# Counting edges with constant tile counts, and attention weights with sources on partitions, in a two-layer graph network

## The reference

```python
h = relu(layernorm(x))
Wh = h @ W.T + b_W;  s_s = Wh @ a_src;  s_d = Wh @ a_dst
e  = leaky_relu(s_s[src] + s_d[dst] + a_b, 0.2)
attn = softmax of e over the edges of each dst
h_prime = segment_sum(attn * Wh[src], dst) + h @ res_W.T + res_b
x = x + gru(h_prime, h)
h = relu(layernorm(x))
for _ in range(4):
    a = segment_sum((h @ W_edge[type].T + b_edge[type])[src], dst)
    h = gru(a, h)
x = x + h
```

## Time and profile before

| | us |
|---|---|
| median of 3 runs | 458.15 (457.98 to 459.03) |
| profiled execution | 458.77 |
| its span, first to last instruction | 456.9 |
| TensorE busy in the span | 391.9 (86%) |
| VectorE busy | 265.6 (58%) |
| ScalarE busy | 160.6 (35%) |
| POOL busy | 98.9 (22%) |

### The profile page before, as it was taken

How to read it: one execution, slowest core, us unless ns; L and a number is a source line. 1 busy time by engine, 2 the same in 40 slices (tenths; PEclk the granted TensorE clock), 3 DMA queues, 4 the chain that set the end, 5 groups by cost and what they waited for, 6 DMA issues and landing times.

```text
span 456.9 us, 8180 instructions
## 1 busy us (share of the span) xinstructions
PE 391.9 (86%) x2544; PEld 280.3 (61%) x2544; DVE 265.6 (58%) x746; ACT 160.6 (35%) x339; POOL 98.9 (22%) x124
## 2 busy tenths in 40 slices
PE   1468856888888889978889999999999999999994
PEld 0365534657777779865337567475674656746693
DVE  6979886776666662576845544444454444544234
ACT  3522118434564654744322232222222222222022
POOL 2101000000000000001007760067700677005500
PEclk9969957888998999999999999999999999999999
DMA  6200000000000000001221331123321233202201
GB/s 154 49 1 1 0 1 0 1 2 1 2 1 2 2 1 1 1 1 47 93 98 47 102 93 71 47 64 99 98 76 47 61 100 100 75 31 74 65 3 32
DMA packets 14500, 19.93 MB, mean 44 GB/s; under 512 B 2591, under 2 KB 7728, under 8 KB 14460
## 3 DMA queue, kind: packets, MB, share of 16 engines
q1 hardware_dynamic: 10276, 12.90, 8.1%
q0 software_dynamic: 2912, 5.97, 5.2%
q10 hardware_dynamic: 1272, 0.54, 0.4%
HBM read 8.27 MB, written 11.13 MB: 42 GB/s over the span
## 4 chain that ended last, share of the span: by engine, by line
PE 72%; DVE 12%; issue 6%; ACT 5%; DVEq 4%; DMA 0%; POOL 0%; SPq 0%; ACTq 0%; POOLq 0%
PE small L1583 26%; PE big L1565 7%; PE small L1447 6%; PE big L1430 6%; PE small L1466 5%; DVE cell_hot L930 3%; PE small L1604 2%; PE small L1617 1%; PE big L1528 1%; DVEq L309 1%; PE small L1528 1%; PE big L1530 1%; PE big L1529 1%; PE small L1519 1%; PE small L1530 1%
## 5 line engine op out<-in xcount | busy, mean ns | idle before, releaser
L1583 PE MATMUL small<-nibbles,store 128*128 128x384 fp8e4 (+1 forms) x640 | 125.8, 353 | 1.4 <-DVE store L1107 0.8
L462 POOL DMA_INDIRECT scores<-messages,w_gat x91 | 88.2, 969 | 120.1 <-DMA messages<-store 93.5
L1583 PEld LDWEIGHTS small<-nibbles,store 128*128 128x128 f16 x640 | 62.3, 98 | 64.4 <-issue 7.3
L930 DVE TENSOR_SCALAR cell_hot<-iota,cell_w,fields 128x320 bf16<-128x320 f16 x264 | 75.1, 357 | 17.1 <-PE big L1430 7.7
L1430 PE MATMUL big<-cell_hot,store 128*128 128x320 bf16 x264 | 56.5, 342 | 20.1 <-DVE cell_hot L930 15.9
L1430 PEld LDWEIGHTS big<-cell_hot,store 128*128 x264 | 35.6, 145 | 36.5 <-issue 32.0
L693 ACT CAST store<-digit_words 128x512 f16<-128x512 f32 x40 | 24.6, 618 | 82.2 <-DVE digit_words L1103 82.2
L1103 DVE TENSOR_TENSOR digit_words<-big,edge_rows 128x512 f32<-128x512 f32 x40 | 27.4, 690 | 40.7 <-PE big L1565 40.7
L1565 PE MATMUL big<-wT,h 128*128 128x512 f32 x80 | 38.6, 599 | 3.0 <-ACT h L689 2.9
L448 POOL TENSOR_TENSOR rstd<-var_e,power 128x2 f32<-128x2 f32 x5 | 3.5, 695 | 140.7 <-DVE var_e L1091 140.7
L1046 DVE SCALAR_TENSOR_TENSOR cell_hot<-rz,cell_hot 128x256 f32<-128x256 f32 (+2 forms) x29 | 11.0, 380 | 38.0 <-ACT cell_hot L664 38.0
(11 more groups left out here) (269 smaller groups left out, 551.8 us busy)
## 6 DMA issues: line engine op xcount, KB each, us to landing
messages<-store SPq DMA_DIRECT2D x40, 256.0 KB, 2.0
scores<-messages,w_gat POOLq DMA_INDIRECT x91, 2.5
xn<-in_x SPq DMA_DIRECT2D x1, 576.0 KB
out<-xn SPq DMA_DIRECT2D x4, 128.0 KB
store<-in_edge_attr SPq DMA_DIRECT2D x1, 256.0 KB
wn<-in_L_gnn_W_edge SPq DMA_DIRECT2D x1, 256.0 KB, 6.4
wn<-in_L_gnn_Wi ACTq DMA_DIRECT2D x1, 192.0 KB, 3.9
wn<-in_L_gnn_Wh_g ACTq DMA_DIRECT2D x1, 192.0 KB, 6.1
```

The costliest lines, as they stand in the source:

```text
L462: g.indirect_dma_start(out=rows16[:, u].rearrange("p a f -> p (a f)"), out_offset=None, in_=table_rows[s % 2][:], in_offset=bass.IndirectO ...
L930: last = v.tensor_scalar(half_hot[:, b * GROUP + q], iota[:, b * HALF:(b + 1) * HALF], cell_w[:, half, bass.ds(tile + q, 1)], fields[:, 1, ...
L1583: last = mm(bank[:, 0:w], m16[s % 2][:, i, t, part], A8[:, t % 2, i, lo:lo + w, t // 2], start=(i == 0 and part == 0 and t == 0), stop=(i ...
```

## The change

The tile count of each of the 40 half windows is now a constant (`TILES`, 231 in all); only the starts are still read from the data, one word for a turn of four half windows. One-hots and matmuls are written out without loops; the ring of eight runs on from half to half; the zero matmuls are gone (the first and last matmul of a half open and close it), and ScalarE's evacuation waits for the count of matmuls (`K.slot`). `cell_w` has four sets instead of two and is filled earlier. `count_turn` swaps the sides: the identity is stationary, digits move in spans of 512 columns, and counts come out with sources on partitions. `weigh` works on sources on partitions, in ten pieces of 128 columns, from `fall` (one column per target, made by a matmul of a new `b_cols`, a Relu and an exponential) and `s_tall` (one number per source). Its result is the stationary side of `aggregate` directly: prob turn and its copy are gone in the fast path. Aggregate J-2 runs in turn J (before, J-3), weigh J-2 right after digits J-1, and the tail is re-ordered to match.

Removed lines that the print above shows are left out where there are more than two on end.

```diff
+TILES = (27, 13, 10, 9, 8, 7, 7, 7, 6, 6, 6, 6) + 8 * (5,) + 2 * (5, 4) + 15 * (4,) + (1,)
+HOTS_BEFORE = (0, *accumulate(TILES))
+AHEAD = 63
+CELL_SETS = 4
...
+        def tile_ranges(eng, J):
+            word = eng.value_load(table[0:1, J:J + 1], min_val=0, max_val=(1 << 26) - 1)
+            first = eng.snap(word & 255)
+            starts = [first]
+            for shift in (8, 14, 20):
+                starts.append(eng.snap(first + ((word >> shift) & AHEAD)))
+            return (starts[0:2], starts[2:4])
+        def window_hots(j, starts):
+            for b, first in enumerate(starts):
+                before = HOTS_BEFORE[2 * j + b]
+                for lo in range(0, TILES[2 * j + b], 2):
+                    tiles = [nc.s_assert_within(first + u, 0, ETP - 1, skip_runtime_bounds_check_because=
+                                                "a start plus its tiles ends within ETP")
+                             for u in range(lo, min(lo + 2, TILES[2 * j + b]))]
+                    yield b, before + lo, tiles
...
+        def weights(n):
+            return exp_b if isinstance(n, int) and n % 2 else exp_a
...
+            for n, run in groupby(range(NS), lambda w: TILES[w]):
+                run = list(run)
+                g.memset(limits[:, run[0]:run[-1] + 1], float(ETP - n)).then_inc(C.limits, len(run))
...
-                act.wait_ge(K.window, 2 * J + half + 1)
+                act.wait_ge(K.slot, HOTS_BEFORE[2 * (2 * J + half + 1)])
...
-            def window_cells(j, half):
-                a.activation(cell_w[:, half], fields[:, 2], ACT.Copy, bias=-float(CELLS * j)).then_inc(K.cellw, 1)
+            def window_cells(j):
+                a.activation(cell_w[:, j % CELL_SETS], fields[:, 2], ACT.Copy,
+                             bias=-float(CELLS * j)).then_inc(K.cellw, 1)
...
-                    if there(J):
-                        window_cells(2 * J + 1, 1)
+                    if 2 * J + 3 < NW:
+                        window_cells(2 * J + 3)
                 if there(J - 3):
...
+                    attn_out(J - 3, J - 3)
+                if J == 1:
+                    falls()
                 if there(J):
                     evac(J, 0)
-                if there(J + 1):
-                    window_cells(2 * J + 2, 0)
+                if 2 * J + 4 < NW:
+                    window_cells(2 * J + 4)
                 if there(J - 1):
                     counts_out(J - 1, count_sum[:, J - 1:J])
                     excesses(J - 1)
+            def falls():
+                act.wait_ge(S0.s_fall, 1)
+                act.wait_ge(S0.d_ps, 1)
+                a.activation(fall[:], smallf[:, 0:NP], ACT.Relu, bias=s_back[:, 0:1], scale=RISE).then_inc(S0.bent, 1)
+                a.activation(s_tall[:], s_up[:], ACT.Exp, scale=RISE / SLOPE)
+                act.wait_ge(S0.bent, 1)
+                a.activation(fall[:], fall[:], ACT.Exp, scale=-1.0).then_inc(S0.fallen, 1)
...
-            a.activation(a_rows[:], ones[:], ACT.Copy, scale=proj[:, 0:1]).then_inc(S0.folded, 1)
+            a.activation(a_rows[:], ones[:], ACT.Copy, scale=proj[:, 0:1])
+            a.activation(b_cols[:], ones[:], ACT.Copy, scale=proj[:, 1:2]).then_inc(S0.folded, 1)
...
+            act.wait_ge(S0.fields, 1)
+            for j in range(CELL_SETS):
+                window_cells(j)
...
-            probs_out(NT - 3)
-            attn_out(NT - 4, NT - 4)
+            attn_out(NT - 3, NT - 3)
             attention_in(0, 0)
             counts_out(NT - 1, count_sum[:, NT - 1:NT])
+            attn_out(NT - 2, NT - 2)
             first_gates(0)
-            attn_out(NT - 3, NT - 3)
-            probs_out(NT - 2)
+            excesses(NT - 1)
+            first_new(0)
             attention_in(1, 1)
...
+            attn_out(NT - 1, NT - 1)
             first_gates(1)
             attention_in(2, 2)
             first_new(1)
             second_norm(0, 0)
             first_gates(2)
             second_h(0, 0)
-            attn_out(NT - 1, NT - 1)
...
-            def one_hots(j, half, tiles_of):
-                first, second, tiles, ahead = tiles_of
+            def one_hots(j, starts):
                 dve.wait_ge(K.cellw, j + 1)
...
+                for b, before, tiles in window_hots(j, starts):
+                    end = before + len(tiles)
+                    if end > RING:
+                        dve.wait_ge(K.slot, end - RING)
+                    for q, tile in enumerate(tiles):
+                        last = v.tensor_scalar(half_hot[:, (before + q) % RING], iota[:, b * HALF:(b + 1) * HALF],
+                                               cell_w[:, j % CELL_SETS, bass.ds(tile, 1)],
+                                               fields[:, 1, bass.ds(tile, 1)], ALU.is_equal, ALU.mult)
+                    last.then_inc(K.pair, len(tiles))
...
-                    dve.wait_ge(S0.s_gain, 1)
+                    dve.wait_ge(S0.fallen, 1)
                 if n >= 2:
...
+                    dve.wait_ge(K.agg, n - 1)
+                for i in range(NT):
+                    last = v.scalar_tensor_tensor(weights(n)[:, i * P:(i + 1) * P], fall[:, n * P:(n + 1) * P],
+                                                  s_tall[:, i:i + 1], count[:, i * P:(i + 1) * P], ALU.max, ALU.mult)
+                last.then_inc(K.probs, 1)
...
-                    one_hots(2 * J, 0, ranges[2 * J])
+                    one_hots(2 * J, ranges[J][0])
+                if J == 3:
+                    reciprocals(0)
                 if there(J - 1):
                     read_digits(J - 1)
+                if there(J - 2):
+                    weigh(J - 2)
                 if there(J):
...
+                    one_hots(2 * J + 1, ranges[J][1])
+                if there(J + 1):
+                    ranges[J + 1] = tile_ranges(dve, J + 1)
+                if J >= 3:
+                    reciprocals(J - 2)
             dve.wait_ge(S0.table, 1)
...
+            ranges = {0: tile_ranges(dve, 0)}
...
             read_digits(NT - 1)
-            reciprocals(NT - 3)
+            weigh(NT - 2)
+            reciprocals(NT - 2)
+            weigh(NT - 1)
             first_front(0)
-            weigh(NT - 1)
+            reciprocals(NT - 1)
             first_back(0)
-            reciprocals(NT - 2)
             layer_sum(0, 0)
             variances(0, 0)
             totals()
             first_front(1)
             second_norm(0, 0)
-            reciprocals(NT - 1)
...
+            def fall_rows():
+                pe.wait_ge(S0.s_rows, 1)
+                for lo, hi in spans():
+                    last = mm(smallf[:, lo:hi], b_cols[:], hT[:, lo:hi], start=True, stop=True)
+                last.then_inc(S0.d_ps, 1)
+            def window(j, half, starts):
                 if later(j, 2):
                     pe.wait_ge(K.evac, j - 1)
...
+                for b, before, tiles in window_hots(j, starts):
+                    end = before + len(tiles)
+                    pe.wait_ge(K.pair, end)
+                    for q, tile in enumerate(tiles):
+                        u = before + q - HOTS_BEFORE[2 * j + b]
+                        last = mm(big[:, 2 * half + b, 0:HALF],
+                                  lane_hot[:, :, bass.ds(tile, 1)].rearrange("p l a -> p (l a)"),
+                                  half_hot[:, (before + q) % RING], start=(u == 0),
+                                  stop=(u == TILES[2 * j + b] - 1), skip_group_check=True)
+                    last.then_inc(K.slot, len(tiles))
             def count_turn(n):
                 pe.wait_ge(K.digits, n + 1)
-                if n >= 2:
-                    pe.wait_ge(K.probsb, n - 1)
+                if n >= 1:
+                    pe.wait_ge(K.counted, n)
                 else:
-                    pe.wait_ge(S0.s_rows, 1)
-                for i in range(NT):
+                    pe.wait_ge(S0.bent, 1)
+                for lo, hi in spans():
                     for q in range(TYPES):
-                        last = mm(smallf[:, i * P:(i + 1) * P], A8[:, q // 2, i, n * P:(n + 1) * P, q % 2], ident16[:],
+                        last = mm(smallf[:, lo:hi], ident16[:],
+                                  A8[:, q // 2, lo // P:hi // P, n * P:(n + 1) * P, q % 2],
                                   start=(q == 0), stop=(q == TYPES - 1), skip_group_check=True)
                 last.then_inc(K.countT, 1)
...
             def aggregate(n):
-                pe.wait_ge(K.probsb, n + 1)
+                fast = isinstance(n, int)
+                if fast:
+                    pe.wait_ge(K.probs, n + 1)
+                else:
+                    pe.wait_ge(K.probsb, n + 1)
                 if later(n):
                     pe.wait_ge(K.attn, n)
+                w = weights(n) if fast else probT
                 for i in range(NT):
-                    last = mm(psD[:, 0:P + 1], probT[:, i * P:(i + 1) * P], Wh[:, i], start=(i == 0),
```

(39 more changed lines are left out.)

128 lines of the change are left out of this document (28 added, 100 removed).

## The result

The changed kernel takes 435.08 us (median of 4 runs, 434.37 to 438.19) against 458.06 on the same chip: ratio 0.951 (95% interval 0.946 to 0.956). It is faster, and 5.6 us slower than forecast. The profiled execution took 434.47 us, its span is 432.3 (before 456.9), TensorE's mean granted clock 0.97.

A forecast was written before the change was run, and what follows sets the result against it. It took one serial chain, TensorE holding 72% and VectorE 12%, as the bound. Gains 6.7 + 3.1 + 2.8 + 13.9 + 0.5 + 2.3 = 29.3, less 0.3 for b_cols, gave 429.5 us; range 422 to 440.

The forecast's parts named there:

- (e): Digits 8 to the last window's end at 172.92: 5 one-hots instead of 8, 6.0 to 5.4 us, gain 0.5.
- (f): Tail to 198.42: two prob turns and one aggregate leave TensorE, some given back; 25.5 to 23.1 us, gain 2.3.
- (a): First turn, 34.7 to 57.96 us: one-hots fall from 80 to 59, each 0.01 cheaper; gain 6.7 us.
- (b): First turn's end to digits 1 at 84.5: ScalarE sets the pace; 26.6 to 23.5 us with 2 for half clock, gain 3.1.
- (c): Digits 1 to digits 2: aggregate 0 pulled in, weigh 0 beside the count turn; 14.8 to 12 us, gain 2.8.
- (d): Six steady turns, digits 2 to 8: weigh beside count turn, one-hots beside aggregate; 67.7 to 53.8 us, gain 13.9.
- Rival 1: Weigh's pieces bind: at 0.28 us each they hold aggregate and VectorE in steady turns and tail, 5.8 us, so 435; chance 0.15.
- Rival 2: TensorE's clock: count turns at half clock in every steady turn, 6 x 1.6 = 10 us, so 440; chance 0.10.
- Rival 3: Steady turns not shortened: table load, reciprocals and register work still stand behind aggregate; (d) gains nothing, 444; chance 0.10.
- Rival 4: Unrolled stream issued too slowly: slower from one-hots 0.40 us apart, about 470 at 0.45; chance 0.04.

## Why the prediction held, and where its sum was off

The forecast of 429.5 was 5.6 low: inside the range of 422 to 440, outside the 423 to 434 that it gave to the forecast's own mechanism. By spans it missed 4.4 (29.0 against 24.6). The other 1.2 is mostly that the profiled execution lay 0.6 above the median before and 0.6 below it after. Two differences of the sum are 0.1 larger than written ((e) 6.0 less 5.4, (f) 25.5 less 23.1). By its steps, forecast and measured gain, a stretch of TensorE ending where its row ends, as in the prediction:

- (a) First turn 6.4 (6.7 less the 0.3 of b_cols), measured 6.7 (to 51.29): the one-hots are 0.274 apart, as priced.
- (b) To digits 1: 3.1, measured 5.5. ScalarE's chain set the pace as followed: the edge weights at 68.24 after 3.50 us of waiting, forecast about 69. Off was the allowance of 2 us for the half clock; the interval was 21.1 against 21.5 without it, though the clock was at half there (granted 0.50 from 68 to 72 us).
- (c) To digits 2: 2.8, measured 1.75. The interval was 13.03; the ring of twelve makes it 11.76, the forecast 12.
- (d) The steady turns: 13.9, measured 8.0. **This is the step that failed**, in its sentence "Windows with more than 8 tiles add 0.275 each". Beyond eight, a tile does not add its one-hot; it waits behind the aggregate for a block and takes the denominator and the next window with it. The three turns forecast at 9.7, 9.4 and 8.9 took 10.94, 10.44 and 10.35; with twelve blocks they take 9.54, 9.11 and 9.07. Of the 5.9 that (d) fell short, 4.0 are the ring (31.73 less 27.72), 1.15 the one turn at half clock, and the rest of 0.75 is the net of turns a little off 8.6. In the turn from 136.23 the count turn is 0.19 over its price, and the aggregate waits 0.28 for weigh, a wait that the sum had put at nothing. Step (a) had reckoned with "the 11 that did not fit in the ring"; step (d) did not.
- (e) 0.5, measured 0.1 (to 150.95), and (f) 2.3, measured 2.8.

That the total missed by less than (d) is luck: (b) gained 2.4 more than forecast and hid part of it.

Rival 1 was half right, and that its 435 is the measured time is luck: of its 5.8 us of weigh an estimated 1.6 came in the steady turns, and the ring's 4.0 and the clock's 1.15 stand in place of the rest. Its price came near (2.9 us, 2.8 elsewhere in the prediction, for the same ten pieces): they take 2.71 us, 0.262 apart, and the statistics instructions at 0.20 were the wrong neighbour. The Trainium skill (VectorE: DVE Perf Modes, "The DRAIN you can't avoid") would have given 2.8 by the sum in the prediction, nearer than my 2.2. Still, each piece lasts 0.348, so the next one does start before that record's end; the section allows this where nothing holds the next instruction. Taking 1.16 us out of each weigh brought 0.6 us a turn, with either ring; the 2.0 us by which the whole stretch fell with the ring of eight hide this, because two of its turns stood at half clock. Rival 2 came in one turn of six, and elsewhere in other executions. Rival 3 did not come: 0.61 us from aggregate to one-hot, forecast 0.9. Rival 4 did not: one-hots no dearer. "Both engines are now at the bound, so nothing hides a further delay" was right of the ring's wait, and cut the other way too: a relief of VectorE paid at once, though only by about half: VectorE already waited 0.41 us for the aggregate in the turn from 136.23.

## What to carry to other kernels

When a change makes the batches of a producer uneven, check each batch against the depth of its buffer: a batch that is one block too long does not cost one more instruction but waits for the consumer's whole queue, and everything in order behind the producer moves with it. Look for such a wait in the timeline of a turn, in front of the batch's last blocks (here 1.10 us), before tuning the instruction beside it. The sum in the producer's group does not tell: it was 15.6 us with the long turns and 13.8 without them. And before a change is judged by a stretch, compare its turns one by one at the same clock. When two parts of a change are timed apart, expect the gains to overlap where both shorten the same turn: 14.9 and 18.4 gave 24.6, and the gap was in the turns that both had shortened.

## What the runs showed of the hardware

Ten 128-column instructions with a scalar per partition cost VectorE 2.71 us, one of 1,280 columns 1.55: 0.13 us for each further start. The half clock came at other places in two executions of one kernel: one count turn of 4.02 us in the fourth steady turn of the one, none there but 3.23 and 3.01 us in the first two of the other. GpSimd's 128-column maximum takes 765 ns, and VectorE's one-hots beside it grew from 357 to 369 ns.
